# Routed tiles of a mixture of experts: rows requested ahead, one dense expert instead of two, and the fill in longer pieces

## The chip, the cores and the metric

The kernel runs on one core of one Trainium2 chip. The metric is the device time of one execution in microseconds (us), the median of the timed runs.

## What is computed

The input x is eight batches of 128 tokens with 128 features. Three steps follow one another.

```python
# 1: one explicit step of a transport and diffusion equation, per batch
x = maximum(x + df * dt, 0)              # df from first and second differences over both axes
# 2: normalisation over features, then over tokens, with scale and shift from a small network
h = layernorm(x) * ln_g + ln_b
h = (h - h.mean(tokens)) * rsqrt(h.var(tokens) + 1e-8)
h = h * gamma[batch] + beta[batch]       # gamma, beta: network of the batch's subject id
# 3: mixture of 8 experts, the best 2 for each of the 1024 tokens
probs = softmax(h @ router_w)
gates, idx = top_k(probs, 2); gates /= gates.sum()
hid  = relu(h @ exp_w1[e] + exp_b1[e])   # 128 to 512
eout = hid @ exp_w2[e] + exp_b2[e]       # 512 to 128
y = sum over the 2 chosen experts of gate * eout
return x + y
```

All values are 32-bit floats.

## The kernel before, in words

Every engine has its instruction list written out by hand, in the functions `sync` (SP), `gpsimd` (POOL), `scalar` (ACT), `tensor` (PE) and `vector` (DVE) inside `build`; semaphores alone order them against each other. The batches are worked on in two halves of four (`HALVES`, `n`).

**Dense and routed experts.** `DENSE = 2` experts are computed for all 1024 tokens: `layer1(e, n, c)` and `layer2(e, n, c)` on PE (L814, L829), `hidden` on ACT (L616), `add_biases` and `add_expert` on DVE (L1138, L1149), with a gate that is zero where the expert was not chosen. The other `ROUTED = 6` experts get only the tokens that chose them, in tiles of 128 rows. Their number must not depend on the data, so `TILES = (2 * 1024 + 6 * 127) // 128 = 21` tiles are always run; the surplus ones work on spare rows.

**Routing.** `logits` (PE L778), `logit_tops`, `choices` and `logit_gap` (DVE L1059 to L1085) find the best two experts of each token; `ranks` (PE L796) counts, with a triangular matrix, how many tokens of the same expert come before; `row_numbers` (DVE L1087) makes of it the row in the DRAM buffer `rows_dram`; `gate_exponent` (ACT L611) and `shares` (DVE L1098) make the two gates; `token_rows` (PE L784, ACT L604) turns h into rows of tokens, `h_row`, with the token's place (column `ID_AT`) and its gate (`GATE_AT`). POOL then scatters them with 16 indirect DMAs (L501), 8 per half, one for each batch and choice. Before that all of `rows_dram` was filled with spare rows: zeros, with a place out of bounds (SP L395, from the tile `spare_row`, which POOL sets at L451 and L484). POOL waits for that fill at L490. `tile_codes` (DVE L1116) computes for each tile one code, which says the expert and the block of 128 rows; SP reads the codes into registers (L402).

**The tile loop.** For tile i SP asks for the expert's weights into one of `W_SLOTS = 5` slots (`tile_weights`, L404; `wt`) and for the rows into one of `ROW_SLOTS = 8` (`tile_rows`, L412; `rt`). PE transposes the rows (L846, into `xT_ps`, which lies in `yt` or `aux`), DVE copies them to `xT_t` (L1207), PE does layer 1 (L855), ACT bias and relu (L669, four instructions a tile), PE layer 2 (L865), DVE gate and bias (L1215 and L1219, result `yg_t`), and POOL scatters the result to `sums_dram` by the tokens' places (L510). On PE the order is layer 1 of tile i, transpose of tile i+1, layer 2 of tile i-1. On DVE it is the copy for tile i+1, then the gating of tile i. A weights slot is free when the tile five back is gated (semaphore `tile_yg`), a row slot when the scatter of the tile eight back has landed (`tile_out`). SP's order is

```python
for i in range(TILES):
    tile_rows(i)
    if i + W_SLOTS - 2 < TILES and i >= 2:
        tile_weights(i + W_SLOTS - 2)
```

**The end.** `sums_dram` (zeroed at L398, one half for the first choice of each token, one for the second) is read back in four pieces of two halves (SP L432), DVE adds both halves to the dense result (L1232, L1233), SP stores each piece (L438).

## Time and profile before

| | |
|---|---|
| median of 2 timed runs | 210.2 us (210.06 to 210.35) |
| the profiled execution, its own time | 211.22 us |
| its span, first to last instruction | 209.4 us |
| PE busy | 132.3 us (63%) |
| DVE busy | 55.0 us (26%) |
| ACT busy | 48.8 us (23%) |
| POOL busy | 46.5 us (22%) |
| moved by DMA | 24.47 MB, mean 117 GB/s |

Times in the profile count from the start of the span. Busy time is that of the instructions of an engine; issuing a DMA is not counted. PE is the matmul part of TensorE, PEld its weight loads. A row of the timeline or of the chain begins with start and duration; in brackets stands the idle time ahead of it and what ended that. "issue" is time in which the engine waited for nothing that the profile shows. The clock column gives TensorE's granted clock as a part of full speed.

### The profile page before, as it was taken

Reading aid. Unit: us, or ns where it says so; the run is one execution under the profiler, and the core shown is the slowest. Engines: PE = TensorE matmul, PEld = TensorE weight load, DVE = VectorE, ACT = ScalarE, POOL = GpSimd, SP = SyncE. Lnnn points to the kernel's source line nnn. Section 1 sums busy time; section 2 is a strip of 40 time slices with the busy share of each in tenths; the row PEclk is TensorE's granted clock in tenths of the full one; section 3 lists DMA queues with packets and bytes.
Section 4 is the critical chain, followed back from the end, with each engine's and each line's share of the span. In section 5 each row is a group of like instructions: output and inputs, shape, how many; then the busy total and the mean of one; then the engine's idle time right before and its main releaser. Section 6 shows DMA issues by size and latency. Waiting matters only on the chain.

```text
span 209.4 us, 2303 instructions
## 1 busy us (share of the span) xinstructions
PE 132.3 (63%) x668; PEld 110.2 (53%) x668; DVE 55.0 (26%) x250; ACT 48.8 (23%) x145; POOL 46.5 (22%) x62
## 2 busy tenths in 40 slices
PE   7999699999304716655675658465746574686400
PEld 3987496886303615545564537454745473575300
DVE  2896673884200201100111011101110111013124
ACT  4356536135000421022202220222022202222200
POOL 4840000677720011101110111011101110112400
PEclk9999969999955785555555555555555555558965
DMA  6918999211791043134412442244224412500054
GB/s 194 341 72 191 155 191 223 87 35 37 235 385 39 0 141 115 28 127 131 131 41 105 133 138 46 96 132 138 45 89 138 131 29 100 153 0 2 0 159 142
DMA packets 17500, 24.47 MB, mean 117 GB/s; under 512 B 1879, under 2 KB 13351, under 8 KB 17488
## 3 DMA queue, kind: packets, MB, share of 16 engines
q1 hardware_dynamic: 15872, 22.54, 39.8%
q0 software_dynamic: 1184, 1.46, 2.0%
q10 hardware_dynamic: 432, 0.34, 0.7%
q8 instruction: 5, 0.08, 0.2%
q14 instruction: 7, 0.06, 0.1%
HBM read 18.04 MB, written 7.28 MB: 121 GB/s over the span
## 4 chain that ended last, share of the span: by engine, by line
DMA 34%; PE 32%; issue 12%; DVE 6%; POOL 6%; SPq 5%; ACT 2%; POOLq 1%; DVEq 0%
DMA rt<-rows_dram 28%; PE zt L865 15%; POOL rows_dram L501 6%; PE zt L855 4%; SPq L408 3%; DVE yg_t L1219 3%; DMA rows_dram<-h_row,row_i 2%; PE yt L846 2%; PE aux L846 2%; PE zt L677 2%; DMA sums<-sums_dram 2%; SPq L432 1%; PE zt L819 1%; PE zt L692 1%; DMA sums_dram<-yg_t,rt 1%
## 5 line engine op out<-in xcount | busy, mean ns | idle before, releaser
L669 ACT ACTIVATE hid_t<-zt,wt 128x128 f32<-128x128 f32 x84 | 24.0, 368 | 120.0 <-PE zt L855 120.0
L855 PE MATMUL zt<-xT_t,wt 128*128 128x128 f32 x168 | 39.9, 413 | 15.8 <-issue 14.9
L510 POOL DMA_INDIRECT sums_dram<-yg_t,rt x21 | 20.4, 972 | 119.0 <-DVE yg_t L1219 118.7
L855 PEld LDWEIGHTS zt<-xT_t,wt 128*128 128x128 f32 x168 | 34.8, 307 | 21.3 <-issue 21.3
L1219 DVE SCALAR_TENSOR_TENSOR yg_t<-zt,rt,b_t 128x128 f32<-128x128 f32 x21 | 7.4, 351 | 112.1 <-PE zt L865 112.1
L865 PE MATMUL zt<-wt,hid_t 128*128 128x128 f32 x168 | 36.6, 393 | 0.0
L865 PEld LDWEIGHTS zt<-wt,hid_t 128*128 128x128 f32 x168 | 34.8, 306 | 0.0
L846 PE MATMUL yt<-ident,rt 128*128 128x128 f32 x11 | 4.8, 436 | 26.6 <-DMA rt<-rows_dram 26.6
L501 POOL DMA_INDIRECT rows_dram<-h_row,row_i x16 | 16.1, 1006 | 6.0 <-issue 4.3
L846 PEld LDWEIGHTS yt<-ident,rt 128*128 128x128 f32 x11 | 1.9, 176 | 29.1 <-DMA rt<-rows_dram 17.8
L846 PE MATMUL aux<-ident,rt 128*128 128x128 f32 x10 | 4.6, 465 | 18.0 <-DMA rt<-rows_dram 18.0
L620 ACT ACTIVATE hid<-zt,we 128x512 f32<-128x512 f32 x16 | 10.9, 689 | 12.7 <-PE zt L819 11.7
L819 PE MATMUL zt<-h,we 128*128 128x512 f32 x30 | 13.7, 592 | 0.0
L846 PEld LDWEIGHTS aux<-ident,rt 128*128 128x128 f32 x10 | 1.9, 193 | 20.2 <-DMA rt<-rows_dram 20.2
L835 PEld LDWEIGHTS yt<-we,hid 128*128 128x128 f32 x64 | 9.0, 226 | 0.5 <-issue 0.5
L835 PE MATMUL yt<-we,hid 128*128 128x128 f32 x64 | 9.1, 311 | 0.0
L819 PEld LDWEIGHTS zt<-h,we 128*128 128x128 f32 x30 | 5.4, 190 | 4.8 <-issue 4.8
L835 PEld LDWEIGHTS aux<-we,hid 128*128 128x128 f32 x64 | 7.4, 192 | 0.5 <-issue 0.5
L835 PE MATMUL aux<-we,hid 128*128 128x128 f32 x64 | 7.6, 276 | 0.0
L1207 DVE COPY xT_t<-yt 128x128 f32<-128x128 f32 x11 | 3.1, 282 | 10.5 <-PE yt L846 10.4
L1215 DVE TENSOR_SCALAR b_t<-wt,rt 128x128 f32<-128x128 f32 x21 | 5.8, 277 | 0.0
L494 POOL COPY h_row<-share 128x8 f32<-128x8 f32 x2 | 0.4, 210 | 20.4 <-DMA rows_dram<-spare_row 20.4
(170 smaller groups left out, 116.4 us busy)
## 6 DMA issues: line engine op xcount, KB each, us to landing
wt<-in_exp_w_dram SPq DMA_DIRECT2D x21, 578.0 KB, 3.9
rows_dram<-spare_row SPq DMA_DIRECT2D x1, 3185.0 KB, 20.7
rt<-rows_dram SPq DMA_DIRECT2D x21, 65.0 KB, 3.5
we<-in_exp_w_dram SPq DMA_DIRECT2D x2, 578.0 KB, 6.9
sums_dram<-zeros SPq DMA_DIRECT2D x2, 512.0 KB, 15.6
sums<-sums_dram SPq DMA_DIRECT2D x8, 128.0 KB, 2.5
f<-in_x_dram SPq DMA_DIRECT2D x2, 256.0 KB, 4.0
ft<-in_x_exchanged_dram SPq DMA_DIRECT2D x2, 256.0 KB, 4.8
```

The lines of the kernel that those rows point to most:

```text
L408: sp.dma_start(wt[:, i % W_SLOTS, :], exp_w[bass.ds(codes[i] >> 3, 1)].rearrange("o p w -> p (o w)")).then_inc(tile_w_in[i % W_SLOTS], 16)
L501: pool.indirect_dma_start(rows_dram, bass.IndirectOffsetOnAxis(ap=row_i[:, b, k:k + 1], axis=0), h_row[:, k, b, :], None, bounds_check=(SP ...
L510: pool.indirect_dma_start(sums_dram, bass.IndirectOffsetOnAxis(ap=rt[:, n, ID_AT:ID_AT + 1].bitcast(I32), axis=0), yg_t[:, n, :], None, bo ...
L620: act.activation(hid[:, c, half(n)], z_d[c], ACT.Relu, bias=we[:, e, B1_AT + c:B1_AT + c + 1]).then_inc(hid_ready, 1)
L669: act.activation(hid_t[:, i % 2, c, :], z_t[i % 2][:, c * P:(c + 1) * P], ACT.Relu, bias=bias).then_inc(tile_hid, 1)
L819: pe.matmul(z_d[c], w1(e, c), h[:, half(n)], start=True, stop=True).then_inc(z_ready, 1)
L835: last = pe.matmul(y_d[e][n][:, k * P:(k + 1) * P], hid[:, c, tok], w2(e, c), start=(c == 0 and k == 0), stop=(c == C - 1), skip_group_che ...
L846: pe.transpose(xT_ps[i % 2], rt[:, i % ROW_SLOTS, 0:P], ident).then_inc(tile_xT_ps, 1)
L855: last = pe.matmul(z_t[i % 2][:, c * P:(c + 1) * P], wt[:, i % W_SLOTS, c * P:(c + 1) * P], xT_t[:, i % 2, :], start=True, stop=True)
L865: last = pe.matmul(y_t[i % 2], hid_t[:, i % 2, c, :], wt[:, i % W_SLOTS, W2_AT + c * P:W2_AT + (c + 1) * P], start=(c == 0), stop=(c == C ...
L1215: then(v.tensor_scalar(b2_t[:, i % 2, :], wt[:, i % W_SLOTS, B2_AT:B2_AT + P], share_t, None, ALU.mult))
L1219: v.scalar_tensor_tensor(yg_t[:, n, :], y_t[i % 2], share_t, b2_t[:, i % 2, :], ALU.mult, ALU.add).then_inc(tile_yg, 1)
```

## The change

`DENSE` goes from 2 to 1, so that expert 1 is routed: seven routed experts, 22 tiles (and codes), 57 blocks of spare rows instead of 49. The remaining dense expert's last-layer additions and the tables follow from it.

The spare rows are filled from a tile `spare_rows` that holds eight rows per partition, so that 56 blocks go out in one DMA with eight rows as one run of 4160 bytes, and the last block in a DMA of its own. The place of the spare rows is set by a memset and no longer copied from the routing constants. SP issues the fill right behind the routing constants.

SP asks for the rows of the first eight tiles at once, and then, for each further tile, for its weights and for the rows of the tile three after it.

PE, ACT and DVE do the routing work of the first half earlier; on PE the logits of both halves move ahead of most layer-1 work. The second choice's half of the sums is read back through ACT's queue.

The diff, without the hunks for tables, constants and the declaration of the tile:

```diff
@@ -28,7 +28,7 @@
 WARM_START = 9
 XN_DVE = 2
 H_DVE = 2
-DENSE = 2
+DENSE = 1
 ROUTED = E - DENSE
 BLOCKS = T // P
 TILES = (TOPK * T + ROUTED * (P - 1)) // P
@@ -38,6 +38,7 @@
 AWAY = 30000.0
 W_SLOTS = 5
 ROW_SLOTS = 8
+FILL = 8
 PIECES = 4
 
 
@@ -387,13 +386,16 @@
             load(pw[:], p64, p64_in)
             load(ident, identity, ident_in)
             load(pv[:], p128, p128_in)
-            for e in range(DENSE):
+            load(we[:, 0], exp_w[ROUTED], w_in[0])
+            load(rc[:], routing, routing_in)
+            sp.wait_ge(fills_ready, 3)
+            whole = SPARE * P
+            sp.dma_start(rows_dram[0:whole].rearrange("(q p j) w -> p q (j w)", p=P, j=FILL),
+                         spare_rows[:].rearrange("p j w -> p (j w)").unsqueeze(1).broadcast_to(
+                             (P, SPARE // FILL, FILL * ROW))).then_inc(filled, 16)
+            sp.dma_start(rows_dram[whole:whole + P], spare_rows[:, 0, :]).then_inc(filled, 16)
+            for e in range(1, DENSE):
                 load(we[:, e], exp_w[ROUTED + e], w_in[e])
-                if e == 0:
-                    load(rc[:], routing, routing_in)
-            sp.wait_ge(fills_ready, 3)
-            sp.dma_start(rows_dram.rearrange("(q p) w -> p q w", p=P),
-                         spare_row[:].unsqueeze(1).broadcast_to((P, SPARE + 1, ROW))).then_inc(filled, 16)
             for k in range(TOPK):
                 sp.dma_start(sums_dram[k * T:(k + 1) * T].rearrange("(p b) d -> p (b d)", p=P),
                              zeros[:]).then_inc(zeroed, 16)
@@ -419,19 +421,19 @@
             for i in range(W_SLOTS):
                 tile_weights(i)
             sp.wait_ge(rows_out, 16 * B * TOPK)
-            for i in range(TILES):
+            for i in range(ROW_SLOTS):
                 tile_rows(i)
-                if i + W_SLOTS - 2 < TILES and i >= 2:
-                    tile_weights(i + W_SLOTS - 2)
+            for i in range(W_SLOTS, TILES):
+                tile_weights(i)
+                if i + ROW_SLOTS - W_SLOTS < TILES:
+                    tile_rows(i + ROW_SLOTS - W_SLOTS)
 
             for i in range(max(0, TILES - ROW_SLOTS), TILES):
                 sp.wait_ge(tile_out[i % ROW_SLOTS], 16 * (i // ROW_SLOTS + 1))
             for n in range(PIECES):
                 two = slice(n * B // PIECES, (n + 1) * B // PIECES)
-                for k in range(TOPK):
-                    sp.dma_start(sums[:, k, two, :],
-                                 sums_dram[k * T:(k + 1) * T].rearrange("(p b) d -> p b d", p=P)[:, two, :]).then_inc(
-                                     sums_in[n], 16)
+                sp.dma_start(sums[:, 0, two, :],
+                             sums_dram[0:T].rearrange("(p b) d -> p b d", p=P)[:, two, :]).then_inc(sums_in[n], 16)
             for n in range(PIECES):
                 two = slice(n * B // PIECES, (n + 1) * B // PIECES)
                 sp.wait_ge(out_ready, n + 1)
@@ -448,7 +450,9 @@
                 ins.then_inc(pool_chain, 1)
                 pool.wait_ge(pool_chain, steps[0])
 
-            pool.memset(spare_row[:], 0.0).then_inc(fills_ready, 1)
+            pool.memset(spare_rows[:], 0.0).then_inc(fills_ready, 1)
+            pool.wait_ge(fills_ready, 1)
+            pool.memset(spare_rows[:, :, ID_AT].bitcast(I32), TOPK * T).then_inc(fills_ready, 1)
             pool.memset(zeros[:], 0.0).then_inc(fills_ready, 1)
             pool.memset(all_ones[:], 1.0).then_inc(before_ready, 1)
             step(pool.iota(row_no[:], pattern=[[0, 1]], base=0, channel_multiplier=1,
@@ -480,14 +484,11 @@
             product(u_b1, ft, gt[:, 0, :]).then_inc(b1_ready[1], 1)
 
             pool.wait_ge(routing_in, 16)
-            pool.wait_ge(fills_ready, 1)
-            pool.tensor_copy(spare_row[:, ID_AT:ID_AT + 1].bitcast(I32),
-                             rc[:, SPARE_AT:SPARE_AT + 1].bitcast(I32)).then_inc(fills_ready, 1)
             pool.tensor_copy(before[:], rc[:, BEFORE_AT:BEFORE_AT + P]).then_inc(before_ready, 1)
             pool.tensor_copy(h_row[:, :, :, ID_AT].bitcast(I32),
                              rc[:, PLACE_AT:PLACE_AT + TOPK * B].bitcast(I32).rearrange(
                                  "p (k b) -> p k b", k=TOPK)).then_inc(places_ready, 1)
-            pool.wait_ge(filled, 16)
+            pool.wait_ge(filled, 32)
             pool.wait_ge(places_ready, 1)
             for n in range(HALVES):
                 pool.wait_ge(share_ready, 2 * (n + 1))
@@ -643,9 +644,9 @@
             normalise(1)
             hidden(0, 0, 2)
             hidden(0, 0, 3)
+            gate_exponent(0)
             inverse_sd_tokens(1)
             conditioned(1)
-            gate_exponent(0)
             hidden(0, 1, 0)
             token_rows(1)
             hidden(0, 1, 1)
@@ -668,6 +669,14 @@
                     bias = wt[:, i % W_SLOTS, B1_AT + c:B1_AT + c + 1]
                     act.activation(hid_t[:, i % 2, c, :], z_t[i % 2][:, c * P:(c + 1) * P], ACT.Relu,
                                    bias=bias).then_inc(tile_hid, 1)
+
+            for i in range(max(0, TILES - ROW_SLOTS), TILES):
+                act.wait_ge(tile_out[i % ROW_SLOTS], 16 * (i // ROW_SLOTS + 1))
+            for n in range(PIECES):
+                two = slice(n * B // PIECES, (n + 1) * B // PIECES)
+                act.dma_start(sums[:, 1, two, :],
+                              sums_dram[T:TOPK * T].rearrange("(p b) d -> p b d", p=P)[:, two, :]).then_inc(
+                                  sums_in[n], 16)
 
         @block.tensor
         def _(pe):
@@ -903,27 +912,30 @@
             pe.wait_ge(net_sb, 6)
             pe.wait_ge(w_in[0], 16)
             layer1_by_pairs()
-            for c in range(1, C):
-                layer1(0, 0, c)
             logits(0)
+            layer1(0, 0, 1)
+            layer1(0, 0, 2)
             token_rows(0)
             pe.wait_ge(xs_ready, BH)
             norm_transposed(1)
+            layer1(0, 0, 3)
             ranks(0)
             pe.wait_ge(h_row_ready, TOPK)
-            for c in range(C):
+            layer2(0, 0, 0)
+            for c in range(1, C):
                 layer2(0, 0, c)
             wait_for_h(1)
+            logits(1)
             layer1(0, 1, 0)
-            logits(1)
             token_rows(1)
-            for c in range(1, C):
-                layer1(0, 1, c)
+            layer1(0, 1, 1)
             ranks(1)
+            layer1(0, 1, 2)
+            layer1(0, 1, 3)
             for c in range(C):
                 layer2(0, 1, c)
-            pe.wait_ge(w_in[1], 16)
             for e in range(1, DENSE):
+                pe.wait_ge(w_in[e], 16)
                 for n in range(HALVES):
                     for c in range(C):
                         layer1(e, n, c)
@@ -1181,11 +1193,11 @@
             normalise(1)
             choices(0)
             logit_gap(0)
+            row_numbers(0)
             moved = token_stats(1)
+            shares(0)
             scale_and_shift(1, moved)
             conditioned(1)
-            row_numbers(0)
-            shares(0)
             logit_tops(1)
             choices(1)
             logit_gap(1)
```

How the order of instructions moves is shown at two places. The first is SP's queue where the tile loop begins; `L408` is a weights request, `L416` a request for rows, and "ISA" the register instruction in front of a request, at which its wait stands. Before:

```order
L408 DMA wt<-in_exp_w_dram 128x1156
L416 ISA [waits rows_out]
L416 DMA rt<-rows_dram 128x130
L416 ISA
L416 DMA rt<-rows_dram 128x130
L416 ISA
L416 DMA rt<-rows_dram 128x130
L408 ISA [waits tile_yg]
L408 DMA wt<-in_exp_w_dram 128x1156
L416 ISA
L416 DMA rt<-rows_dram 128x130
```

Now, from the last of the eight first requests for rows (`L410` is a weights request, `L418` one for rows):

```order
L418 ISA
L418 DMA rt<-rows_dram 128x130
L410 ISA [waits tile_yg]
L410 DMA wt<-in_exp_w_dram 128x1156
L418 ISA [waits tile_out0]
L418 DMA rt<-rows_dram 128x130
L410 ISA [waits tile_yg]
L410 DMA wt<-in_exp_w_dram 128x1156
L418 ISA [waits tile_out1]
L418 DMA rt<-rows_dram 128x130
```

Before, the fourth request for rows stood behind a wait for a gated tile; now the first such wait stands behind eight requests. The wait for a landed scatter (`tile_out`) is met from the ninth request on in both, and in the new order it stands between the weights of tiles 5 and 6, where the old one had it first behind the weights of tile 10.

The second place is PE between the first half's layer 1 and its layer 2 (`zt0<-h,we` and `zt1<-h,we` are layer 1, `yt<-pv,h` the logits, `yt<-ident,h` the token rows, `aux<-ident,xn` the second half's norm transposes, `yt<-mask` the ranks). Before:

```order
L826 MATMUL zt0<-h,we 128x256 x2
L819 MATMUL zt1<-h,we 128x512
L819 MATMUL zt0<-h,we 128x512
L819 MATMUL zt1<-h,we 128x512
L781 MATMUL yt<-pv,h 128x8 x4
L787 MATMUL yt<-ident,h 128x128 x4
L770 MATMUL aux<-ident,xn 128x128 x4
L804 MATMUL yt<-mask,before 128x32
```

Now:

```order
L835 MATMUL zt0<-h,we 128x256 x2
L790 MATMUL yt<-pv,h 128x8 x4
L828 MATMUL zt1<-h,we 128x512
L828 MATMUL zt0<-h,we 128x512
L796 MATMUL yt<-ident,h 128x128 x4
L779 MATMUL aux<-ident,xn 128x128 x4
L828 MATMUL zt1<-h,we 128x512
L813 MATMUL yt<-mask,before 128x32
```

The logits moved ahead of three layer-1 matmuls; the last of these moved behind the norm transposes and in front of the ranks.

## Rows read from the trace of the kernel before

**Rows 1.** The page, its first line.

```profile
span 209.4 us, 2303 instructions
```

**Rows 2.** Waits of SP: waiter, releaser, us in total, times, longest.

```profile
SPq L408 <- DVE yg_t L1219: 97.2, 16, 7.3
```

**Rows 3.** Chain of waits over one tile: start us, us, what.

```profile
135.27 0.36 DVE yg_t L1219
...
136.34 3.61 DMA rt<-rows_dram
...
142.32 0.36 DVE yg_t L1219
```

**Rows 4.** Chain of waits over the last tiles.

```profile
189.03 0.79 issue
...
191.95 0.98 issue
...
196.28 0.13 POOL sums_dram L510
```

**Rows 5.** Timeline of VectorE over the last tiles.

```profile
184.42 0.35 DVE L1219 SCALAR_TENSOR_TENSOR yg_t<-zt,rt,b_t 128x128 f32<-128x128 f32 x1 [6.30 <-PE zt L865]
...
189.17 0.35 DVE L1219 SCALAR_TENSOR_TENSOR yg_t<-zt,rt,b_t 128x128 f32<-128x128 f32 x1 [4.01 <-PE zt L865]
...
192.09 0.35 DVE L1219 SCALAR_TENSOR_TENSOR yg_t<-zt,rt,b_t 128x128 f32<-128x128 f32 x1 [2.18 <-PE zt L865]
...
195.09 0.35 DVE L1219 SCALAR_TENSOR_TENSOR yg_t<-zt,rt,b_t 128x128 f32<-128x128 f32 x1 [2.07 <-PE zt L865]
...
196.00 0.35 DVE L1219 SCALAR_TENSOR_TENSOR yg_t<-zt,rt,b_t 128x128 f32<-128x128 f32 x1 [0.36 <-PE zt L865]
```

**Rows 6.** Stretches: span, busy (count) of PE, PEld, DVE, ACT, POOL; clock, DMA share, GB/s.

```profile
72.00:180.00 108.00, 64.53 (x263) 56.04 (x263) 11.73 (x48) 17.15 (x60) 15.55 (x16) 0.52 0.34 101
...
189.00:196.00 7.00, 5.10 (x42) 4.74 (x41) 2.12 (x8) 2.29 (x8) 1.94 (x2) 0.95 0.01 1
```

**Rows 7.** Timeline where the tile loop begins.

```profile
65.35 0.45 PE L846 MATMUL yt<-ident,rt 128*128 128x128 f32 x1 [11.17 <-DMA rt<-rows_dram]
...
71.86 0.35 DVE L1219 SCALAR_TENSOR_TENSOR yg_t<-zt,rt,b_t 128x128 f32<-128x128 f32 x1 [2.80 <-PE zt L865]
```

**Rows 8.** DMAs to landing: fill (KB, us), weights, scatter of results.

```profile
rows_dram<-spare_row SPq DMA_DIRECT2D x1, 3185.0 KB, 20.7
...
DMA to landing us min/median/max: 3.5/3.9/8.6
...
DMA to landing us min/median/max: 2.1/3.6/5.0
```

**Rows 9.** Timeline of POOL, around the scatters of rows.

```profile
36.59 0.20 POOL L494 COPY h_row<-share 128x8 f32<-128x8 f32 x1 [20.37 <-DMA rows_dram<-spare_row]
...
58.14 0.97 POOL L501 DMA_INDIRECT rows_dram<-h_row,row_i  x1 [0.30 <-issue]
```

**Rows 10.** SP: reading the codes (durations ns, first and last start), then asking for weights.

```profile
L402 SPq TENSOR_LOAD <-code x21: 266/271/463, 39.9 to 51.4; - x21
...
52.56 2.87 SPq L408 DMA_DIRECT2D wt<-in_exp_w_dram  x5
```

**Rows 11.** Stretches, columns as in rows 6: first weights; reading back the sums.

```profile
58.00:63.00 5.00, 0.00 (x0) 0.00 (x0) 0.00 (x0) 0.00 (x0) 0.97 (x1) 0.50 0.93 375
...
201.00:206.00 5.00, 0.00 (x0) 0.00 (x0) 2.50 (x6) 0.00 (x0) 0.00 (x0) 0.50 0.78 242
```

**Rows 12.** Timeline of VectorE, the second share of the first half.

```profile
30.49 0.16 DVE L1105 TENSOR_TENSOR share<-ex,share 128x4 f32<-128x4 f32 x1
```

**Rows 13.** SP: reading back the sums (durations ns, first and last start).

```profile
L432 SPq DMA_DIRECT2D sums<-sums_dram x8: 332/432/433, 199.7 to 202.9; - x8
```

**Rows 14.** The page, groups: relu on ACT and scatter on POOL (busy, mean ns).

```profile
L669 ACT ACTIVATE hid_t<-zt,wt 128x128 f32<-128x128 f32 x84 | 24.0, 368 | 120.0 <-PE zt L855 120.0
...
L510 POOL DMA_INDIRECT sums_dram<-yg_t,rt x21 | 20.4, 972 | 119.0 <-DVE yg_t L1219 118.7
```

More of the change, by code:

```diff
@@ L64 @@
 PLACE_AT = BASE_AT + E
-SPARE_AT = PLACE_AT + TOPK * B
-FIRST_ROW_AT = SPARE_AT + 1
+FIRST_ROW_AT = PLACE_AT + TOPK * B
 AHEAD_AT = FIRST_ROW_AT + SPARE
@@ L101, in routing_constants @@
     out[:, PLACE_AT:PLACE_AT + TOPK * B] = place.reshape(P, TOPK * B).astype(np.int32).view(np.float32)
-    out[:, SPARE_AT] = np.full(P, TOPK * T, np.int32).view(np.float32)
     expert, block = np.divmod(np.arange(SPARE), BLOCKS)
@@ L227, in build @@
         code = sb("code", [P, 1], I32)
-        spare_row = sb("spare_row", [P, ROW])
+        spare_rows = sb("spare_rows", [P, FILL, ROW])
         zeros = sb("zeros", [P, T])
```

## Prediction, made before the changed kernel had run

> **What bounds the kernel now.** The profiled execution took 211.2 us, of which the span is 209.4 us [rows 1]; some 1.8 us lie around it. The two timed runs gave 210.2 us in the middle, 1.0 us less. I read the waits of SP's queue first, then the chain of waits over one tile, then the same chain over the last tiles, then the granted clock.
>
> The chain that ended last runs through the routed tiles from 65 to 196 us, nearly two thirds of the span. SP waited 97.2 us in 16 waits for the gated rows of the tile before the last one (L408) [rows 2]. The chain over one tile shows what this costs: VectorE writes yg_t at 135.27, SP asks for weights and then, at 136.34, for rows, the rows take 3.61 us, TensorE transposes and finishes the older tile, and the next yg_t comes at 142.32 [rows 3]. A tile takes 7.05 us, and TensorE waits for 65 KB of rows that queue behind 578 KB of weights, although eight row slots exist.
>
> The last tiles were not asked for late: their rows were there. Their chain has no DMA in it [rows 4], and VectorE writes yg_t at 184.42, 189.17, 192.09 and 195.09, then 196.00 [rows 5]: 4.75 us at half clock, then 2.92 and 3.00 us at full clock. So the trace holds the new loop in small. Between L865 and the next L855 stands 0.79 to 0.98 us "issue" [rows 4]: yg_t and the copy of the next transposed tile on VectorE, one behind the other. The change leaves that gap in place.
>
> **The rows asked for ahead.** The change takes the wait for yg_t from in front of the row requests: SP asks for eight tiles of rows at once, and afterwards for rows three tiles ahead of the weights. The loop then costs what the last tiles cost, provided three things hold.
>
> *The clock.* From 72 to 180 us the granted clock was 0.52 (1.2 GHz, with one short stretch at 2.4) while TensorE was busy 64.5 of 108 us. From 189 to 196 us it was 0.95, so 2.4 GHz, after two tiles that ran without a wait, and it stayed there across the gap of 0.98 us [rows 4, 6]. TensorE works 2.0 of every 3.0 us there. I take full clock, with 0.95 us of caution for some late rises.
>
> The Trainium skill ("TensorE: Matmul & The Clock Gate", the section on a second HAM failure mode: psum-queue depth-cycling) speaks against this: a kernel whose TensorE idles briefly but often between groups of matmuls was seen to swing between the clocks. By it the loop would lie anywhere between the two sums below; by the last three tiles it lies at the lower. Three tiles are little evidence, and this is the second rival.
>
> *The weights.* Tile i's weights are asked for once tile i-5 is gated, now behind a row request that waits for the scatter of tile i-6 (i+2-8). A scatter landed 2.1 to 5.0 us after its start, median 3.6; weights took 3.5 to 8.6, median 3.9 [rows 8]. From yg_t to a scatter's start are 1.2 us (195.09 to 196.28) [rows 4, 5]; two issues I put at 1.0, twice the 0.47 between issues in [rows 13]. So weights i land about 1.2 + 3.6 + 1.0 + 3.9 = 9.7 us after the yg_t of tile i-6. Their L855 starts 0.85 us after the yg_t of tile i-2, that is 4 x 3.0 + 0.85 = 12.9 us after the same point. Slack 3.2 us: no wait. Their traffic of 0.72 MB per tile at 3.05 us is 236 GB/s, and 375 GB/s was moved in 58 to 63 us [rows 11].
>
> *The other engines.* ACT has 24.0 / 21 = 1.14 us of L669 and POOL 0.97 us of scatter per tile, even with 0.3 us between, both under 3 [rows 14].
>
> Loop: from the first transpose at 65.35 [rows 7] to the first yg_t at 71.86 are 6.5 us, kept. Then 20 periods to the 21st yg_t. I take 3.0 for each (60.0), plus the 0.95, then 0.91 for the last tile and 0.35 for its write: 68.7 us for 22 tiles, against 131.0 for 21 (65.35 to 196.35). The 22nd tile is in it, at one period. Saved: 62.3 us. Bounds: 2.92 per tile and no late rise gives 66.2; the half-clock period of 4.75 throughout gives 6.5 + 95 + 2.3 = 103.8.
>
> **The fill, the routing and the dense expert.** POOL waited 20.37 us for the fill of rows_dram and could start only at 36.59, although the first shares were there at 30.65 (30.49 and 0.16) [rows 9, 12]. The fill moved 3185 KB in pieces of 520 bytes in 20.7 us [rows 8]. Now it moves 3705 KB in pieces of 4160 bytes, asked for at about 6 us instead of 15.85, because it no longer waits for routing constants and a copy behind POOL's products. At the 375 GB/s of [rows 11] this is 10 us and over by about 21 us; even at the old rate, 158 GB/s, it would be over by 34. The longer memset ahead of it costs POOL about what the one of zeros does, and lies in front of a wait for its first load: nothing. POOL then starts on the shares. TensorE's logits come three layer-1 matmuls earlier, but ranks follow the norm transposes and one layer-1 matmul, and shares(0) stands behind token_stats(1), delayed by the row numbers: I put shares(0) at 29.6, one us before the old time, and the scatters 6.8 us earlier than before, the last at 51.4 instead of 58.14 [rows 9].
>
> That gain is not the loop's. SP reads the tile codes at 0.6 us each (21 from 39.9 to 52.5) and asks for five weights from 52.56 [rows 10]; rows now stand behind all five in SP's queue. The second half's ranks come about 0.8 us earlier, since TensorE is then held by the same layer-2 group; one more code costs 0.6. So weights from about 52.3, their 2.96 MB at 375 GB/s with 1 us to start until 61.2, and the first rows at 61.6. That replaces 65.35: 3.7 us saved. Bounds: 0 if the codes come 2 us later, as much as the second half's statistics are put back, and scatters slow the weights as before; 5 if the codes come 1 us sooner still.
>
> The second dense expert goes at no gain: TensorE stood idle 11.17 us for rows after it [rows 7], and the code reads and weights, which set the start, wait for the ranks alone. Its price is the 22nd tile, already counted.
>
> **The end.** SP issued the eight sums pieces from 199.7 to 202.9 [rows 13]. Half of them now go through ACT's queue, so the last is issued 4 x 0.47 = 1.9 us sooner. The DMA share there was 0.78 at 242 GB/s [rows 11]: the 1.05 MB take 4.3 us so, and 3.4 at full share, 0.9 less. I take 1.4, halfway between the two, bounds 0 and 1.9. The end from the last yg_t (196.35) to 209.4 was 13.05, now 11.65.
>
> The Trainium skill ("DMA: Bandwidth & Descriptors", rules for kernel authors) says that a second issuing engine adds no bandwidth and only saves issue time. By the rule taken strictly the saving would lie between the two prices just given, since both are issue time; by a queue of its own for ACT it could be more, which the share of 0.78 speaks against.
>
> **Sum.** 61.6 + 68.7 + 11.65 = 141.95 us span; 1.8 around it gives 143.75 against 211.2 profiled; 210.2 / 211.2 of it, 143.0 us, stands beside the median of the runs.
>
> **The rivals.**
> *Half clock or swinging clock.* With brief idling at every tile the clock does not hold. For it: 0.52 over 108 us. Against: those gaps are 2 us and more, and the last tiles. All at half: 61.6 + 103.8 + 11.65 + 1.8, less 0.8, is 178 us; half of the loop so, 160.
> *Weights become the wait.* Scatters at 5.0 and weights at 8.6 us: 1.2 + 5.0 + 1.0 + 8.6 to land, then L855, transpose, older L865, gap, L855, transpose, L865 (about 6.0) to yg_t; 21.8 over six tiles is 3.6 us a tile, loop 81, time 155. Medians speak against it, the heavier traffic for it.
> *Slower than before.* The same ring with the scatter wait in front of every weights request. The loop must pass 131 us, so over 6.1 us per tile, which needs 37 us over six tiles against 15.7 at medians (1.2 + 3.6 + 1.0 + 3.9 + 6.0): scatter and weights together above 28 us where their maxima give 13.6. Then 212 us or more.
> *The rows do not come ahead*: each later request still waits for its slot's scatter. That scatter is of a tile eight back, and the old order already carried this wait, so nothing supports it; it would give 131 + 7.05 = 138 us of loop and 212 us.
>
> **Chances.** Forecast 0.76; clock 0.13; weights 0.08; rows not ahead 0.01; slow ring 0.02. The range goes from 136 (2.92 a tile, 5 us at the start, 1.9 at the end) to 166, past the weights case and a loop that is half-clocked for half its length. Two per cent, 4 us, is about what a measurement tells from no change; only the last two cases come near: faster 0.97, same 0.02 (rows not ahead and half of the slow ring), slower 0.01.
>
> **What would show it.** Right: yg_t every 2.9 to 3.1 us, granted clock near 1 from some 8 us after the first transpose, no wait of TensorE for rows or weights, first transpose near 61.6, the fill landed before 22, scatters from 31. Wrong: a clock that drops inside the loop, waits of L855 for weights, or SP held by scatters for longer than a period.

## The result, and the profile after

| | before | changed |
|---|---|---|
| median of the timed runs | 210.2 us | 144.2 us (143.48 to 144.89, 2 runs) |
| ratio | | 0.686, 95% interval 0.671 to 0.700 |
| the profiled execution, its own time | 211.2 us | 144.9 us |
| its span | 209.4 us | 142.8 us |
| first transpose of a tile | 65.35 | 62.79 |
| tile loop, to the end of the last yg_t | 131.0 us, 21 tiles | 68.1 us, 22 tiles |
| from there to the end | 13.05 us | 11.95 us |

A second set of runs of the same kernel, `changed_again`, taken beside two of the experiments below, gave 144.6 us (143.73 to 145.62, 4 runs) and a ratio of 0.690 (0.675 to 0.705). Medians and spreads here take in all runs of a kernel, ratios and their intervals only those within 1.5% of its fastest run. The prediction was 143.0 us with a range of 136 to 166.

The first lines of the page of the changed kernel (busy us, share of the span, instructions) and the row of the granted clock in 40 slices:

```profile
span 142.8 us, 2173 instructions
...
PE 87.2 (61%) x605; PEld 74.1 (52%) x605; DVE 51.2 (36%) x237; ACT 44.4 (31%) x141; POOL 48.3 (34%) x63
...
PEclk9999999599999555555699999999999999999855
```

TensorE's busy time fell from 132.3 to 87.2 us although the tiles are one more. Two things are in this. In `order_only` below, which has exactly the matmuls of the kernel before, it is 98.8 us: 33.5 us less, because most of them ran at 1.2 GHz before and run at 2.4 there. The other 11.6 us are the matmuls of the second dense expert, less those of the 22nd tile.

The chain of waits from the first request for rows to the third tile (start us, us, what) answers to [rows 3, 7]:

```profile
55.28 7.38 DMA rt<-rows_dram
...
62.79 0.46 PE yt L855
...
63.71 2.05 PE zt L864 x8
...
66.44 2.04 PE zt L864 x8
...
70.28 0.96 issue
71.24 1.13 PE zt L864 x8
...
72.48 0.89 PE zt L874 x8
73.37 0.76 issue
74.13 1.13 PE zt L864 x8
```

In [rows 3] each period held a request and 3.61 us of DMA. Here DMA stands once, at the start, for 7.38 us, and then come only TensorE's two groups and the 0.76 us in which VectorE gates one tile and copies the next. L864 takes 2.05 us for the first two tiles and 1.13 from the third on: the clock rose between them.

The timeline of VectorE at the first two results, in the middle and at the last two answers to [rows 5]:

```profile
70.39 0.35 DVE L1231 SCALAR_TENSOR_TENSOR yg_t<-zt,rt,b_t 128x128 f32<-128x128 f32 x1 [3.89 <-PE zt L874]
...
73.48 0.35 DVE L1231 SCALAR_TENSOR_TENSOR yg_t<-zt,rt,b_t 128x128 f32<-128x128 f32 x1 [2.15 <-PE zt L874]
...
99.57 0.35 DVE L1231 SCALAR_TENSOR_TENSOR yg_t<-zt,rt,b_t 128x128 f32<-128x128 f32 x1 [2.18 <-PE zt L874]
...
102.49 0.35 DVE L1231 SCALAR_TENSOR_TENSOR yg_t<-zt,rt,b_t 128x128 f32<-128x128 f32 x1 [2.18 <-PE zt L874]
...
129.59 0.35 DVE L1231 SCALAR_TENSOR_TENSOR yg_t<-zt,rt,b_t 128x128 f32<-128x128 f32 x1 [2.06 <-PE zt L874]
...
130.50 0.35 DVE L1231 SCALAR_TENSOR_TENSOR yg_t<-zt,rt,b_t 128x128 f32<-128x128 f32 x1 [0.36 <-PE zt L874]
```

The period is 2.89 to 2.92 us nearly everywhere; over the 20 periods from 70.39 to 129.59 it is 2.96. In the trace of `changed_again` the same 20 periods are 2.91 each:

```profile
71.96 0.35 DVE L1231 SCALAR_TENSOR_TENSOR yg_t<-zt,rt,b_t 128x128 f32<-128x128 f32 x1 [3.96 <-PE zt L874]
...
130.18 0.35 DVE L1231 SCALAR_TENSOR_TENSOR yg_t<-zt,rt,b_t 128x128 f32<-128x128 f32 x1 [2.07 <-PE zt L874]
```

One row for the stretch of the loop (columns as in [rows 6]) shows the clock at full speed throughout, with 41.4 us of matmuls in 57:

```profile
72.00:129.00 57.00, 41.37 (x333) 38.25 (x332) 14.11 (x57) 21.98 (x78) 19.00 (x20) 1.00 0.69 209
```

What SP waits for has changed place. Its waits (in total, times, longest), which answer to [rows 2]:

```profile
SPq L418 <- DMA sums_dram<-yg_t,rt: 29.4, 13, 4.0
...
SPq L410 <- DVE yg_t L1231: 11.8, 2, 11.3
```

The 97.2 us on gated tiles became 11.8, of which 11.3 is the wait for the first tile; in their place SP waits 29.4 us for scatters in front of its row requests. Nobody but the later weights waits behind it, and they are late at two tiles:

```profile
PE yt L855 <- DMA rt<-rows_dram: 22.0, 1, 22.0
PE zt L864 <- issue: 14.1, 18, 1.0
PE zt L864 <- DMA wt<-in_exp_w_dram: 2.5, 2, 1.4
```

2.5 us of waits for weights in 22 tiles. Each stands in place of an "issue" gap of 0.8 us, so that the loss is 0.9 us: two periods of 3.54 and 3.24 us where the others have 2.92. It does not come in every execution: in `changed_again` no period is longer than 3.09 us, and its one wait put down to weights is 0.8 us, no more than the gap. The chain names one of the two, from a scatter of 6.09 us at 109.51 through a row request at 115.79 to weights of 4.86 us from 116.66:

```profile
109.51 6.09 DMA sums_dram<-yg_t,rt
115.79 0.33 SPq L418
...
116.66 4.86 DMA wt<-in_exp_w_dram
121.57 1.16 PE zt L864 x8
```

Weights landed later under the denser traffic. Here are weights and scatters to landing (minimum, median, maximum), against medians of 3.9 and 3.6 in [rows 8]:

```profile
DMA to landing us min/median/max: 3.8/5.2/7.8
```
```profile
DMA to landing us min/median/max: 2.1/4.2/6.1
```

For the weights this holds in every trace below with the new order: the medians are 4.7 to 5.6 us. For the scatters it is less firm: 3.7 in `changed_again`, and 3.1 to 4.7 in the others.

### The profile page after: what moved, and what is told of

Same layout as the page of the kernel before. It is cut to its first block, busy times and chain, and to the rows that moved or that the text cites. A ratio compares the mean times of both kernels' runs of the same rounds, so it can differ in the third digit from the quotient of the medians.

```text
span 142.8 us, 2173 instructions
## 1 busy us (share of the span) xinstructions
PE 87.2 (61%) x605; PEld 74.1 (52%) x605; DVE 51.2 (36%) x237; ACT 44.4 (31%) x141; POOL 48.3 (34%) x63
## 4 chain that ended last, share of the span: by engine, by line
PE 45%; DMA 17%; issue 15%; SPq 9%; DVE 8%; ACT 3%; ACTq 1%; POOLq 0%; POOL 0%; DVEq 0%
PE zt L864 16%; PE zt L874 11%; SPq L404 7%; DMA sums_dram<-yg_t,rt 6%; DMA rt<-rows_dram 5%; PE zt L828 3%; DMA wt<-in_exp_w_dram 3%; PE zt L686 3%; DMA sums<-sums_dram 3%; SPq L410 2%; PE zt L701 2%; PE yt L855 1%; PE zt L835 1%; PE aux L855 1%; PE aux L746 1%
## 5 line engine op out<-in xcount | busy, mean ns | idle before, releaser
L511 POOL DMA_INDIRECT sums_dram<-yg_t,rt x22 | 21.3, 970 | 59.2 <-DVE yg_t L1231 58.9
L864 PE MATMUL zt<-xT_t,wt 128*128 128x128 f32 x176 | 26.7, 298 | 17.5 <-issue 14.1
L864 PEld LDWEIGHTS zt<-xT_t,wt 128*128 128x128 f32 x176 | 22.9, 203 | 21.5 <-issue 16.7
L874 PE MATMUL zt<-wt,hid_t 128*128 128x128 f32 x176 | 23.8, 281 | 0.0
L874 PEld LDWEIGHTS zt<-wt,hid_t 128*128 128x128 f32 x176 | 22.2, 198 | 0.0
L828 PE MATMUL zt<-h,we 128*128 128x512 f32 x14 | 7.5, 640 | 0.0
L621 ACT ACTIVATE hid<-zt,we 128x512 f32<-128x512 f32 x8 | 5.5, 690 | 4.5 <-PE zt L828 3.8
L844 PE MATMUL yt<-we,hid 128*128 128x128 f32 x32 | 5.0, 330 | 0.0
L844 PEld LDWEIGHTS yt<-we,hid 128*128 128x128 f32 x32 | 4.8, 244 | 0.0
L686 PE MATMUL zt<-warm 128*128 128x512 bf16 x9 | 4.0, 628 | 1.2 <-DVE warm L974 1.2
L844 PE MATMUL aux<-we,hid 128*128 128x128 f32 x32 | 3.7, 275 | 0.0
```

Source lines behind the costliest of these rows:

```text
L511: pool.indirect_dma_start(sums_dram, bass.IndirectOffsetOnAxis(ap=rt[:, n, ID_AT:ID_AT + 1].bitcast(I32), axis=0), yg_t[:, n, :], None, bo ...
L686: pe.matmul(warm_ps, warm[:, 0:P], warm[:], start=True, stop=True)
L828: pe.matmul(z_d[c], w1(e, c), h[:, half(n)], start=True, stop=True).then_inc(z_ready, 1)
L844: last = pe.matmul(y_d[e][n][:, k * P:(k + 1) * P], hid[:, c, tok], w2(e, c), start=(c == 0 and k == 0), stop=(c == C - 1), skip_group_che ...
L864: last = pe.matmul(z_t[i % 2][:, c * P:(c + 1) * P], wt[:, i % W_SLOTS, c * P:(c + 1) * P], xT_t[:, i % 2, :], start=True, stop=True)
L874: last = pe.matmul(y_t[i % 2], hid_t[:, i % 2, c, :], wt[:, i % W_SLOTS, W2_AT + c * P:W2_AT + (c + 1) * P], start=(c == 0), stop=(c == C ...
```

## The experiments

"Changed" means the changed kernel; where a time is compared, the base is its 144.2 us (144.6 in the second set).

### The order of the requests alone, and everything but the order

`order_only` is the kernel before with this one edit; `old_order` is the changed kernel with the reverse edit.

```diff
-            for i in range(TILES):
-                tile_rows(i)
-                if i + W_SLOTS - 2 < TILES and i >= 2:
-                    tile_weights(i + W_SLOTS - 2)
+            for i in range(ROW_SLOTS):
+                tile_rows(i)
+            for i in range(W_SLOTS, TILES):
+                tile_weights(i)
+                if i + ROW_SLOTS - W_SLOTS < TILES:
+                    tile_rows(i + ROW_SLOTS - W_SLOTS)
```

> The kernel before with SP's order of requests in the tile loop alone changed (eight requests for rows at once, then weights i and rows i+3); two dense experts, 21 tiles, old fill, old routing order. Theory (the order of SP's requests carries the whole gain): the first transpose stays at about 65.4 us, since the last scatter of rows still lands at 63.3; yg_t then comes every 2.9 us as in the changed kernel, loop 68.1 - 2.9 = 65.2 us, end 13.05 as before: span about 143.6, time about 145 us, within 1.5 us of the changed kernel. Rival (fill, routing and the dense expert carry part of it): 150 us or more, with a first transpose later than 66 or a period above 3.1.

> The changed kernel with SP's old order of requests in the tile loop, all else as changed. Theory: first transpose near 62.8 as in the changed kernel, then the old period of 7.05 us at half clock for 22 tiles, 131 + 7 = 138 us of loop, end 12: span about 213, time about 214 us, slower than before by one tile less the earlier start. Rival: the other parts help the loop too, and it lies below 205.

`order_only` took 142.55 us (141.36 to 143.12, 4 runs; ratio 0.676, 0.668 to 0.683), `old_order` 216.9 us (one run), 6 us above the kernel before and near the 214 expected. The first and the last results of `order_only`, and its first transpose:

```profile
71.57 0.35 DVE L1221 SCALAR_TENSOR_TENSOR yg_t<-zt,rt,b_t 128x128 f32<-128x128 f32 x1 [3.53 <-PE zt L867]
...
74.46 0.35 DVE L1221 SCALAR_TENSOR_TENSOR yg_t<-zt,rt,b_t 128x128 f32<-128x128 f32 x1 [2.15 <-PE zt L867]
...
127.81 0.35 DVE L1221 SCALAR_TENSOR_TENSOR yg_t<-zt,rt,b_t 128x128 f32<-128x128 f32 x1 [0.36 <-PE zt L867]
```
```profile
64.33 0.44 PE L848 MATMUL yt<-ident,rt 128*128 128x128 f32 x1 [9.58 <-DMA rt<-rows_dram]
```

From 71.57 to 126.91 (0.90 before the last) are 19 periods at 2.91 us. So the order of SP's requests alone gives the whole gain, by the medians some 2 us more than the change as a whole; all other parts together are worth nothing or cost those 2 us. (The intervals of the ratios overlap, so the 2 us are not shown as the gain is.) The rival, that they carry part of it, falls. In `old_order` the first transpose stood at 62.81 and the last result at 202.14, with this row for 72 to 195 us:

```profile
72.00:195.00 123.00, 73.55 (x301) 64.18 (x302) 13.36 (x54) 20.58 (x72) 16.78 (x19) 0.52 0.32 99
```

### How much of the old period was the clock

`old_order_warm` adds matmuls of zeros to `old_order`, whose result nobody reads:

```diff
+                if i > 0:
+                    for _ in range(12):
+                        pe.matmul(yt[:, half(0)], warm[:, 0:P], warm[:], start=True, stop=True,
+                                  skip_group_check=True)
                 if i + 1 < TILES:
                     tile_transposed(i + 1)
```

> The changed kernel with SP's old order of requests and with 12 matmuls of zeros (128x512, bf16, result unused) on TensorE in front of each transpose from the third on, in the time in which it waits for rows. Tells how much of the old 7.05 us per tile is the clock and how much the wait. Theory: the clock holds at 2.4 GHz, the chain yg_t, request, rows (4.6 us together) stays, transpose and layer 2 shrink from 2.2 to 1.1: 5.9 to 6.0 us per tile, about 195 us against 216.9. Rival (the clock was the main loss): below 170 us; or the matmuls themselves hold up the transpose: no faster than 212.

It took 207.5 us (one run) against 216.9. The clock was held at 2.4 GHz over the whole stretch, as this row shows against the one above (0.52):

```profile
72.00:195.00 123.00, 99.28 (x584) 63.62 (x592) 15.83 (x63) 22.88 (x80) 20.75 (x22) 1.00 0.33 100
```

and two results in the middle lie 5.91 us apart; the 20th and the 21st of the 22 lie 5.40 apart:

```profile
127.56 0.35 DVE L1233 SCALAR_TENSOR_TENSOR yg_t<-zt,rt,b_t 128x128 f32<-128x128 f32 x1 [5.41 <-PE zt L872]
...
133.47 0.35 DVE L1233 SCALAR_TENSOR_TENSOR yg_t<-zt,rt,b_t 128x128 f32<-128x128 f32 x1 [5.17 <-PE zt L872]
...
186.80 0.35 DVE L1233 SCALAR_TENSOR_TENSOR yg_t<-zt,rt,b_t 128x128 f32<-128x128 f32 x1 [4.76 <-PE zt L872]
...
192.20 0.35 DVE L1233 SCALAR_TENSOR_TENSOR yg_t<-zt,rt,b_t 128x128 f32<-128x128 f32 x1 [4.66 <-PE zt L872]
```

The period came out as expected (5.97 on average), the time did not (195 expected). Where the rows are waited for, over the first 17 periods, `old_order` takes 7.00 us each and this run 6.06. The last three periods have no such wait, and there the added matmuls only hold up the transpose: 5.5, 5.5 and 5.4 us, against 4.75, 4.76 and 2.8 in `old_order`. The first result too came 2.9 us later behind them. So the 9 us between the two times understate the clock: 17 times 0.94 us make 16, of which the added matmuls took back 4.1 at the end and 2.9 at the start. Per waiting tile this leaves 0.9 us for the clock alone and 3.1 (6.06 less 2.96) for the wait. The new order gains 72 us and brings the clock with it. Both kernels were run once only; the periods are read from their traces.

### Two dense experts instead of one

```diff
-DENSE = 1
+DENSE = 2
```

> The changed kernel with DENSE = 2: expert 1 dense again, 21 tiles and codes, 49 blocks of spare rows, all else as changed. Theory (the second dense expert lies in time in which TensorE waits for rows anyway, so routing it costs one tile and one code read): TensorE is done with it near 55 us, the first rows come near 62, the loop is one period (2.9) shorter and starts 0.6 earlier: about 3.5 us less than the changed kernel, 140.7 us. Rival (routing it pays, because the dense work holds up codes, clock or DMA): equal to the changed kernel or slower, with a first transpose after 63.

139.8 us (139.66 to 140.75, 4 runs; ratio 0.665, 0.658 to 0.671), 4.4 to 4.8 less than the changed kernel. TensorE's first transpose:

```profile
62.36 0.44 PE L855 MATMUL yt<-ident,rt 128*128 128x128 f32 x1 [6.98 <-DMA rt<-rows_dram]
```

It comes 0.4 us earlier than in the changed kernel (1.9 earlier than in `changed_again`), after 6.98 us of waiting where the changed kernel waits 22.0. The dense expert had lain in idle time, and routing it costs a tile of 2.9 us, a code read, and some of the clock at the start of the loop: from the first transpose to the first result are 6.98 us here, 7.60 and 7.66 in the two traces of the changed kernel, because the clock rose sooner (from 68 to 71 us the granted clock was 0.95 here, 0.67 and 0.50 there). The 0.9 us for late weights is lost in one of these two traces only. So this part of the change makes the kernel slower, by a measured 4 us and more.

### The sums through one queue

```diff
-            for i in range(max(0, TILES - ROW_SLOTS), TILES):
-                act.wait_ge(tile_out[i % ROW_SLOTS], 16 * (i // ROW_SLOTS + 1))
-            for n in range(PIECES):
-                ...
-                act.dma_start(sums[:, 1, two, :],
```

SP issues both halves again.

> The changed kernel with all eight pieces of the sums read back through SP's queue again, as before. Theory: SP's issues at 0.47 us each set the end; the span from the last yg_t to the end grows by 1.1 us (from 11.95 to 13.05), about 145.3 us. Rival (the engines set it, a second queue gives nothing): within 0.3 us of the changed kernel.

145.45 us (144.92 to 146.72, 4 runs). The end, from the last yg_t on, was 12.83 us (130.37 to 143.2) against 11.95: 0.9 us, between the two theories. SP's eight issues, against four and four side by side in the changed kernel:

```profile
133.74 3.65 SPq L436 DMA_DIRECT2D sums<-sums_dram  x8
```
```profile
134.23 1.76 SPq L435 DMA_DIRECT2D sums<-sums_dram  x4
134.24 1.80 ACTq L677 DMA_DIRECT2D sums<-sums_dram  x4
```

In the times alone, 0.9 us lies within the spread of the runs; the traces carry it, and not to the tenth. The same stretch is 12.54 us in `order_only` and 13.05 in the kernel before, both with one queue, and 12.16 in `changed_again`; over all traces here with two queues it is 11.65 to 12.4. The difference of the means is 0.7 us.

### What sets the start of the loop

`codes_split`:

```diff
-            codes = [sp.value_load(...) for i in range(TILES)]
+            read_codes(W_SLOTS)
             for i in range(W_SLOTS):
                 tile_weights(i)
+            read_codes(15)
             sp.wait_ge(rows_out, 16 * B * TOPK)
...
             for i in range(W_SLOTS, TILES):
                 tile_weights(i)
+                read_codes(i + 11)
```

> The changed kernel, but SP reads five codes, asks for the five weights, reads ten more codes, waits for the scattered rows and asks for eight tiles of rows; the other codes are read one per tile in the loop. Theory (the start of the loop is set by 22 code reads and by the five weights that rows queue behind, and not by the scatters, which land near 54): weights asked for from 42, landed by 51, rows asked for at 54, first transpose near 56 in place of 62.8; loop 68 and end 12 as before: about 137.5 us. Rival (the scatters or the weights set the start): first transpose after 60, above 141 us.

138.2 us (137.15 to 139.43, 4 runs; ratio 0.659, 0.653 to 0.666). SP's queue and the first transpose in the changed kernel, then here:

```profile
52.14 2.94 SPq L410 DMA_DIRECT2D wt<-in_exp_w_dram  x5
55.28 4.19 SPq L418 DMA_DIRECT2D rt<-rows_dram  x8
```
```profile
42.22 2.64 SPq L417 DMA_DIRECT2D wt<-in_exp_w_dram  x5
54.51 4.05 SPq L425 DMA_DIRECT2D rt<-rows_dram  x8
```
```profile
56.47 0.45 PE L864 MATMUL yt<-ident,rt 128*128 128x128 f32 x1 [15.50 <-DMA rt<-rows_dram]
```

The weights are asked for 10 us earlier, the rows at 54.51, when the last scatter has landed, and they land in 2 us instead of 7.4. So in the changed kernel the scatters were not the limit; the code reads and the weights in front of the rows were (which of these two more was not taken apart). The earlier fill and the earlier routing brought the start of the last scatter from 58.14 to 51.49, and only here does most of that reach the loop: the first transpose stood at 65.35 before, at 64.33 in `order_only`, at 62.79 and 64.30 in the two traces of the changed kernel. Neither the fill nor the routing was taken out by itself.

`two_dense_codes` is the same with `DENSE = 2`.

> The changed kernel with DENSE = 2 and the codes read as in codes_split. Theory: the dense expert ends near 55 us on TensorE, the first rows come near 56, so that it just hides, and TensorE comes into the loop at full clock: the first yg_t then lies about 5 us after the first transpose instead of 7.6. Against the run with two dense experts (139.8 us) 6 us for the start and 2.5 for the clock: about 131.5 us. Rival: dense work holds the start back (add_expert, the weights' slots), or the clock falls anyway: above 135 us.

133.1 us (132.70 to 133.45, 4 runs; ratio 0.637, 0.632 to 0.641). The dense work does hide: the transpose came at 56.41 after a wait of 1.35 us for VectorE. But the first result came 6.3 us after it and not 5. The clock fell once more, in the very stretch of the first tiles:

```profile
56.00:59.00 3.00, 1.64 (x11) 1.30 (x11) 1.06 (x5) 0.59 (x3) 0.00 (x0) 0.96 0.55 130
59.00:62.00 3.00, 3.00 (x14) 3.00 (x15) 0.00 (x0) 1.51 (x7) 0.00 (x0) 0.50 0.10 25
```

TensorE had been busy 2.05 and 1.64 of 3 us in the two stretches before 59 us. In `all_three` below, with the same start and 2.42 and 1.54 us busy in those stretches, the clock stayed up (4.7 us to the first result), as its row for the same stretch shows; in `all_four` it fell (7.6 us).

```profile
59.00:62.00 3.00, 2.96 (x26) 2.99 (x27) 0.83 (x3) 1.84 (x7) 0.00 (x0) 1.00 0.18 43
```

What brings it down in one execution and not in the other was not settled.

### What holds the period at 2.9 us

`copy_first` lets VectorE copy tile i+2 before it gates tile i:

```diff
             tile_columns(0)
+            tile_columns(1)
             for i in range(TILES):
-                if i + 1 < TILES:
-                    tile_columns(i + 1)
+                if i + 2 < TILES:
+                    tile_columns(i + 2)
                 tile_gated(i)
```

> The changed kernel with VectorE's copy of the transposed tile i+2 in front of the gating of tile i, so that the next layer 1 need not wait for yg_t and the copy. Theory of the ring (weights i wait for tile i-5's gating and stand behind a row request that waits for tile i-6's scatter, at the measured medians 4.2 and 5.2 us): TensorE's own 2.2 us per tile cannot be reached, the period stays at about 2.8 and layer 1 now waits for weights: 142 us. Rival (only VectorE's order held the period): 2.2 to 2.3 us per tile, 131 us or less.

137.8 us (135.44 to 139.12, 4 runs; ratio 0.651, 0.643 to 0.660): between the two. Its waits of TensorE and one row of its loop:

```profile
PE zt L864 <- DMA wt<-in_exp_w_dram: 9.2, 11, 2.5
```
```profile
90.00:102.00 12.00, 9.71 (x81) 9.00 (x79) 4.12 (x14) 5.39 (x20) 4.85 (x5) 1.00 0.88 284
```

The first results came 1.5 and 1.9 us apart, so TensorE's own work is 1.9 us a tile and not 2.2, and the average is 2.48: the order on VectorE had held the period, and now late weights do. Late because they are asked for late, or because 0.72 MB per tile at 284 GB/s take 2.5 us? `copy_slots` gives ten row slots and keeps the requests, so that a row request waits for an older scatter:

```diff
-ROW_SLOTS = 8
+ROW_SLOTS = 10
...
-            for i in range(ROW_SLOTS):
+            for i in range(W_SLOTS + 3):
                 tile_rows(i)
             for i in range(W_SLOTS, TILES):
                 tile_weights(i)
-                if i + ROW_SLOTS - W_SLOTS < TILES:
-                    tile_rows(i + ROW_SLOTS - W_SLOTS)
+                if i + 3 < TILES:
+                    tile_rows(i + 3)
```

> copy_first (the changed kernel with VectorE's copy ahead of the gating) with ten row slots in place of eight and the same requests, so that a row request waits for the scatter of tile i-7 and no longer for that of tile i-5. In copy_first layer 1 waited 9.2 us for weights and a tile took 2.48 us. Theory of the ring (weights are late because they are asked for behind the wait for a scatter): that wait goes, 2.2 us per tile, about 132 us, few waits for weights. Rival (the DMA engines are the limit: 0.72 MB per tile moved at 285 GB/s is 2.5 us, at a DMA share of 0.89): the period stays at 2.4 to 2.5 and the share goes up little, 136 to 138 us, layer 1 still waits for weights.

128.15 us (127.87 to 131.44, 4 runs; ratio 0.611, 0.592 to 0.631). The same two views:

```profile
PE zt L864 <- DMA wt<-in_exp_w_dram: 2.9, 4, 1.3
```
```profile
90.00:102.00 12.00, 11.31 (x101) 11.12 (x100) 4.96 (x18) 6.59 (x24) 4.96 (x6) 1.00 0.96 333
```

2.9 us of waits instead of 9.2, 2.09 us per tile instead of 2.48, 333 GB/s instead of 284. The requests were late; the DMA engines could give more, and at a share of 0.96 they are now near their end.

### All together

`all_three` joins `two_dense_codes` and `copy_first`; `all_four` adds the ten slots of `copy_slots`.

> The changed kernel with two dense experts, the codes read in parts (as in two_dense_codes) and VectorE's copy ahead of the gating (as in copy_first). The three savings touch different places (the hidden dense work, the start of the loop, the period) and add up if that is right: 133.1 less 6.4 (144.2 to 137.8 for copy_first, with one tile less: 6.1): about 127 us. Rival (weights for 21 tiles in a shorter time are limited by DMA, or the dense work now stands in the way): above 130.

> all_three with ten row slots as in copy_slots: two dense experts, codes read in parts, VectorE's copy first, row requests behind an older scatter. Theory (in all_three layer 1 waited 10.6 us for weights asked for behind the wait for a recent scatter): first yg_t at 61.3 as in all_three, then 19 tiles at 2.1 us (copy_slots had 41.8 us for 20 periods), 0.9 and the end of 12: about 114 us of span, 116 us. Rival (the DMA engines, 0.94 to 0.96 busy in copy_slots, are now the limit, with the code reads between the requests): above 120.

126.4 us (124.54 to 127.17, 4 runs; ratio 0.598, 0.576 to 0.621) and 117.2 us (114.78 to 117.52, 4 runs, against 210.5 for the kernel before, timed beside it). The sums come out, each with some luck in its parts. In `all_three` the first result came 1.4 us earlier than in `two_dense_codes`, because the clock stayed up, and 19 periods of 2.66 us saved 4.8 us more, where 6.1 were expected of the loop; layer 1 waited 10.6 us for weights. In `all_four` the first result came at 64.17 and not at 61.3, because the clock fell, and the periods were shorter than the 2.1 us expected. Its first and its last result:

```profile
64.17 0.35 DVE L1240 SCALAR_TENSOR_TENSOR yg_t<-zt,rt,b_t 128x128 f32<-128x128 f32 x1 [1.29 <-PE zt L883]
...
103.20 0.35 DVE L1240 SCALAR_TENSOR_TENSOR yg_t<-zt,rt,b_t 128x128 f32<-128x128 f32 x1 [0.36 <-PE zt L883]
```

19 periods in 38.1 us (to 102.29, the last result but one), 2.01 each, and TensorE waited for weights once, 0.2 us.

## Why the prediction was right

**The rows asked for ahead** was the step that carried it, and it held in kind and size: 68.1 us of loop against 68.7. Two terms in it were off and in part cancelled. "6.5 us, kept" from the first transpose to the first yg_t measured 7.6 (7.7 in `changed_again`): the clock rose later after the transpose, so that the second layer 1 took 2.04 us where it took 1.74 before, and the first layer 2 1.78 where it took 1.06. The 20 periods measured 59.2 us against 60.95. Reading the period off the last three tiles of the old trace, which ran as all tiles do now, was the right source; `order_only` shows that nothing else was needed.

**The clock.** 1.00 from 72 to 129 us: it did not swing, with gaps of 0.76 us in every 2.9. The swinging clock that the Trainium skill ("TensorE: Matmul & The Clock Gate", a second HAM failure mode: psum-queue depth-cycling) tells of, in a kernel that idles briefly and often, does not appear inside this loop. The forecast had the price of the clock for a tile without a wait (4.75 us against 2.92) and none for a tile that waits for its rows: there it is 0.9 us.

**The weights.** "Slack 3.2 us: no wait" was too good. It rested on the old medians of 3.9 and 3.6 us, which were 5.2 and 4.2 in this trace. The ring was right: the medians took up 1.9 us of the slack, and slow scatters the rest at two tiles, at a price of 0.9 us; in `changed_again` (4.8 and 3.7) nothing was lost. That the allowance of 0.95 us, made for the clock, was about this much is luck. Two of the signs named for being wrong did appear in small: L864 waited for weights, and SP was held by scatters for up to 4.0 us, longer than a period. Neither moved the time by more than that 0.9 us.

**The fill, the routing and the dense expert.** The fill was issued at 5.71 and landed 14.0 us later, its last block (issued at 6.31) 15.0 us later, at 21.3 and so before 22 as said. The working does not give that: 6 and 10 us are 16 and not 21, and the traffic ahead of the fill had no term. It came out by a surplus of 5 us that the text does not explain. The first row scatter started at 31.35 and the last at 51.49 (said: 31 and 51.4); weights were asked for at 52.14 (52.3). That this gain is not the loop's was the point of that part, and `codes_split` shows it. The first transpose came at 62.79 and not 61.6: the step that was mis-sized is "their 2.96 MB at 375 GB/s with 1 us to start". From the first weights request to the first rows were 10.5 us, not 9.3. In `changed_again` the first transpose came at 64.30, so the "3.7 us saved" were 2.6 and 1.0. "Its price is the 22nd tile" was right as far as it went; the measured price of routing the dense expert was 4.4 to 4.8 us, of which the tile is 2.9 and the slower first two tiles are 0.6.

**The end.** 1.1 us were saved instead of 1.4, of which `sums_on_sp` puts 0.9 down to the second queue, and the means of all traces 0.7: near the lower of the two prices. (The prediction says that both prices are issue time; the 0.9 was worked out from the DMA share.) The Trainium skill ("DMA: Bandwidth & Descriptors", rules for kernel authors) says that a second issuing engine saves issue time and adds no bandwidth. The traces agree: SP's issues took 1.76 us instead of 3.65, and the 5 us from 135 on moved 259 GB/s here and 242 in `sums_on_sp`.

**The sum.** 62.8 + 68.1 + 11.95 = 142.8 against 61.6 + 68.7 + 11.65 = 141.95. The errors are +1.2, -0.6 and +0.3. The lower end of the range, 136, is not what its three terms give: 60.35 + 66.2 + 11.15 + 1.8, less 0.8, is 138.7 us.

## What to carry to other kernels

Where slots are free and an engine still waits for a transfer, look at what stands in front of the request in the issuing queue: a wait put there for another tile's buffer delays every request behind it, and moving it was worth 68 us here with no byte less to move. A prologue or an epilogue that runs without the wait shows in the old trace what the loop will cost without it. And price each part of a bundle: here one edit gave the whole gain, one cost 4 us, and an earlier start of the scatters lay mostly unused behind the next limit.

## What the hardware showed that I had not expected

- The landing times of the weights rose well before the DMA engines were full: at a mean share of 0.69 in the loop (against 0.34 before) their median went from 3.9 to 5.2 us (4.8 in `changed_again`).
- The clock held at 2.4 GHz through a loop with TensorE busy 73% of the time, in regular gaps of 0.76 us; in the old order it stayed at 1.2 GHz over nearly the whole loop at 60% busy, with two gaps in each tile, of 2.0 and 0.8 us. Whether the busy share or the longer gap made the difference was not tried.
- With the same start, the clock fell at the first tiles in two kernels and not in a third, worth up to 2.9 us from the transpose to the first result (4.7, 6.3 and 7.6 us).
